# Ranks of two edge sorts: products on TensorE in place of scans on VectorE

## The reference

```python
agg = segment_sum(h_src * attn_weights[:, None], tgt, num_segments=N)      # layer 0, by target
return segment_sum(proj, src, num_segments=n_nodes)                       # layer 1, by source
out = segment_sum(h[src] * alpha[:, :, None], dst, num_segments=N)        # layer 2, by target
mat = mat.at[i].set(c * ri - s * rj); mat = mat.at[j].set(s * ri + c * rj)  # layer 3, edge by edge
return x @ mat.T
```

## Time and profile before

| | |
|---|---|
| median of three runs | 7119.62 us (7114.62 to 7124.22) |
| the profiled execution | 7110.56 us, span 7108.8 us |
| DVE busy, share of the span | 5179.6 us, 73% |
| PE busy | 4283.0 us, 60% |
| POOL busy | 4285.9 us, 60% |
| ACT busy | 1186.0 us, 17% |

### The profile page before, as it was taken

How to read it: one execution, slowest core, us unless ns; L and a number is a source line. 1 busy time by engine, 2 the same in 40 slices (tenths; PEclk the granted TensorE clock), 3 DMA queues, 4 the chain that set the end, 5 groups by cost and what they waited for, 6 DMA issues and landing times. The chain is left out here.

```text
span 7108.8 us, 179388 instructions
## 1 busy us (share of the span) xinstructions
PE 4283.0 (60%) x60437; PEld 3470.5 (49%) x60555; DVE 5179.6 (73%) x12108; ACT 1186.0 (17%) x2828; POOL 4285.9 (60%) x3974
## 2 busy tenths in 40 slices
PE   0000288885425554888887788886888875355541
PEld 0000166663214443677775677764777754233331
DVE  6999877776545556688874688865788855588877
ACT  0000022220011110122220122210222211222210
POOL 5888777776357760477760677741777720677720
PEclk9999999996555556999998999998999987555555
DMA  0000000001044441677722677614777500444420
GB/s 30 1 4 1 1 1 1 1 1 27 11 104 131 131 117 40 196 216 209 211 72 79 194 218 208 193 34 124 208 215 210 149 19 28 96 111 110 111 58 18
DMA packets 708570, 691.60 MB, mean 97 GB/s; under 512 B 234981, under 2 KB 589355, under 8 KB 708165
## 3 DMA queue, kind: packets, MB, share of 16 engines
q0 software_dynamic: 227328, 446.06, 23.1%
q1 hardware_dynamic: 480846, 240.51, 12.2%
HBM read 766.03 MB, written 77.58 MB: 119 GB/s over the span
## 5 line engine op out<-in xcount | busy, mean ns | idle before, releaser
L1671 POOL DMA_INDIRECT kvring<-kvtab,oth x1776 | 1800.4, 1014 | 818.7 <-issue 432.3
L1069 POOL DMA_INDIRECT e_hg<-htab,oth_d x992 | 1012.6, 1021 | 818.7 <-issue 763.6
L1722 PE MATMUL ea_pss<-ea_qb,ea_kT 128*128 128x128 f32 x7104 | 1016.4, 276 | 0.0
L1722 PEld LDWEIGHTS ea_pss<-ea_qb,ea_kT 128*128 128x128 f32 x7104 | 942.4, 193 | 16.0
L1766 ACT ACTIVATE ea_kT<-ea_pst 128x512 f32<-128x512 f32 x888 | 482.0, 595 | 1833.9 <-PE ea_pst L1710 1833.9
L1710 PE MATMUL ea_pst<-ident,kvring 128*128 128x128 f32 x3552 | 484.8, 280 | 306.5 <-DMA kvring<-kvtab,oth 304.6
L241 POOL DMA_INDIRECT steps<-or_rec,or_rplacei x392 | 567.1, 1447 | 135.2 <-issue 121.5
L1806 DVE TENSOR_REDUCE ea_sc<-ea_pss 128x64 f32<-128x1024 f32 x444 | 540.3, 1217 | 47.0 <-PE ea_pss L1722 47.0
L1710 PEld LDWEIGHTS ea_pst<-ident,kvring 128*128 128x128 f32 x3552 | 384.1, 141 | 379.2 <-DMA kvring<-kvtab,oth 213.6
L1834 DVE TENSOR_TENSOR ea_mix<-ea_hot,ea_psg 128x1024 f32<-128x1024 f32 (+1 forms) x444 | 542.2, 1221 | 0.2
L1719 PE MATMUL ea_pss<-mrow,ea_mk 128*128 128x256 bf16 x1776 | 490.2, 276 | 58.0 <-ACT ea_kT L1766 25.7
(11 more groups left out here) (506 smaller groups left out, 8295.2 us busy)
## 6 DMA issues: line engine op xcount, KB each, us to landing
ea_qb<-qtab SPq DMA_DIRECT2D x1776, 64.0 KB
qtab<-at_qst SPq DMA_DIRECT2D x75, 512.0 KB, 3.3
kvring<-kvtab,oth POOLq DMA_INDIRECT x1776
e_stack<-ohtab SPq DMA_DIRECT2D x744, 32.0 KB
kvtab<-at_kvst SPq DMA_DIRECT2D x75, 256.0 KB, 2.7
e_hg<-htab,oth_d POOLq DMA_INDIRECT x992
ea_mk<-mtab SPq DMA_DIRECT2D x444, 3.0 KB
htab<-Hd SPq DMA_DIRECT2D x2, 3200.0 KB, 11.9
```

Of the source, the lines that this page charges most:

```text
L1069: pool.indirect_dma_start(out=hg[:, b % RING, u, :], out_offset=None, in_=htab, in_offset=bass.IndirectOffsetOnAxis(ap=oth[:, b * 4 + u:b ...
L1671: pool.indirect_dma_start(out=kv[:, b % R, u, :], out_offset=None, in_=kvtab, in_offset=bass.IndirectOffsetOnAxis(ap=oth[:, b * QB + u:b * ...
L1722: mm = pe.matmul(ps_s[r % 2][:, u, k * 2 * HN:(k + 1) * 2 * HN], kT[:, r % 2, u, k, :], qb[:, r, u, :], start=False, stop=True, skip_group ...
```

## The change

Both sorts get their ranks from PE.

The first sweep still makes one mask for each block on DVE, now as bf16 (`hot`). For every mask PE forms one product of 392 columns with `colsel`, a matrix whose only column of ones stands so that block u's counts by column land in row u of a PSUM bank; 64 blocks share a bank and are summed there (two banks in turn). After 64 blocks DVE scans the bank once along the columns (`columns`), so 2 scans for the target sort and 4 for the source sort give, for each block, the edges in all earlier columns. The first place of the block is added as a column (`bcol`, turned by a small product), and the sum is split in two bf16 parts (`rows`).

In the second sweep DVE makes the mask, PE forms two products of 392 columns that add up in one PSUM bank, `laterb` by mask (the edges of this block in earlier partitions of the same column) and a selector by `rows` (the block's row, spread over the partitions), and DVE copies the sum, predicated by the mask, from PSUM into the places. Three PSUM banks and three mask buffers are used in turn. Constants for this are set by `sort_constants` on DVE and `sort_selectors` on ACT. `PARTS` becomes (232, 40, 120). The order of the edges within a block is now by columns.

```diff
-PARTS = (272, 32, 88)
+CH = 64
+MIDDLE = 32768.0
+PARTS = (232, 40, 120)
...
+def sort_constants(dve, K, B, s):
+    link = linker(dve, s["sconst"])
+    link(dve.memset(B["colsel"][:, :], 0.0))
+    for at in (CH - 1, 2 * CH - 1):
+        link(dve.memset(B["colsel"][:, at:at + 1], 1.0))
...
+def sort_selectors(act, B, s):
+    act.wait_ge(s["eye2"], 1)
+    act.activation(B["selb"][:, :, :], B["eye2"][:, :].unsqueeze(2).broadcast_to([P, CH, P]), ACT.Copy).then_inc(s["selb"], 1)
...
+    def columns(c):
+        dve.wait_ge(s["cnt"], min(SB, CH * (c + 1)))
+        dve.tensor_tensor_scan(E[:, c, 1:RT], K["ones"][:, 0:1].broadcast_to([P, RT - 1]), ps_c[c % 2][:, 0:RT - 1], 0.0,
+                               ALU.mult, ALU.add).then_inc(s["run"], 1)
...
-        dve.scalar_tensor_tensor(out=run[:, b % 3, :], in0=blk[:, :], scalar=float(b),
+        dve.scalar_tensor_tensor(out=hot[:, b % 3, :], in0=blk[:, :], scalar=float(b),
                                  in1=K["ones"][:, 0:1].broadcast_to(full), op0=ALU.is_equal, op1=ALU.mult,
-                                 accum_out=cnt[:, b:b + 1]).then_inc(s["cnt"], 1)
+                                 accum_out=cnt[:, b:b + 1]).then_inc(s["here"], 1)
+        if b >= CH + 2 and b % CH == 2:
+            columns(b // CH - 1)
...
+    for c in range(NC):
+        link(dve.tensor_scalar(rows[:, c, :], E[:, c, :], bcol[:, c:c + 1], None, ALU.add))
+        dve.scalar_tensor_tensor(out=rows[CH:P, c, :], in0=E[CH:P, c, :], scalar=bcol[CH:P, c:c + 1], in1=rows[CH:P, c, :],
+                                 op0=ALU.add, op1=ALU.subtract).then_inc(s["rows"], 1)
+
     for k in range(SB + 2):
         if k < SB:
             if k >= 3:
                 dve.wait_ge(s["put"], k - 2)
-            dve.tensor_scalar(here[:, k % 3, :], blk[:, :], float(k), None, ALU.is_equal).then_inc(s["here"], 1)
-        if 1 <= k < SB + 1:
-            b = k - 1
-            dve.wait_ge(s["here"], b + 1)
-            dve.tensor_tensor_scan(run[:, b % 3, :], K["ones"][:, 0:1].broadcast_to(full), here[:, b % 3, :],
-                                   til[:, 3, b:b + 1], ALU.mult, ALU.add).then_inc(s["run"], 1)
+            dve.tensor_scalar(hot[:, k % 3, :], blk[:, :], float(k), None, ALU.is_equal).then_inc(s["here"], 1)
         if k >= 2:
             b = k - 2
-            dve.wait_ge(s["run"], b + 1)
+            dve.wait_ge(s["rank"], b + 1)
             if b >= 1:
                 dve.wait_ge(s["put"], b)
-            dve.copy_predicated(place[:, :], here[:, b % 3, :].bitcast(I32), run[:, b % 3, :]).then_inc(s["put"], 1)
+            dve.copy_predicated(place[:, :], hot[:, b % 3, :].bitcast(I16), ps_k[b % 3][:, 0:RT]).then_inc(s["put"], 1)
...
-def sort_offsets(pe, K, B, s):
-    SB, cnt = B["SB"], B["cnt"]
-    pe.wait_ge(s["cnt"], SB)
-    pe.matmul(B["ps_o"][:, 0:SB], K["later"][:, :], cnt[:, :], start=True, stop=True)
+def sort_ranks(pe, K, B, s, selectors):
+    SB, NC, cnt, hot, ps_c, ps_k = (B[n] for n in ("SB", "NC", "cnt", "hot", "ps_c", "ps_k"))
+    for b in range(SB):
+        c, u = b // CH, b % CH
+        pe.wait_ge(s["here"], b + 1)
+        if u == 0 and c >= 2:
+            pe.wait_ge(s["run"], c - 1)
+        pe.matmul(ps_c[c % 2][:, 0:RT], B["colsel"][:, CH - 1 - u:CH - 1 - u + P], hot[:, b % 3, :], start=(u == 0),
+                  stop=(u == CH - 1 or b == SB - 1)).then_inc(s["cnt"], 1)
     pe.matmul(B["ps_n"][:, 0:SB], K["ones"][:, :], cnt[:, :], start=True, stop=True).then_inc(s["offs"], 1)
...
+    for b in range(SB):
+        c, u = b // CH, b % CH
+        if u == 0:
+            pe.wait_ge(s["rows"], c + 1)
+        pe.wait_ge(s["here"], SB + b + 1)
+        if b >= 3:
+            pe.wait_ge(s["put"], b - 2)
+        pe.matmul(ps_k[b % 3][:, 0:RT], B["laterb"][:, :], hot[:, b % 3, :], start=True, stop=False)
+        pe.matmul(ps_k[b % 3][:, 0:RT], B["selb"][:, u, :], B["rows"][:, c, :], start=False, stop=True).then_inc(s["rank"], 1)
```

More of the change, by code:

```diff
@@ L11 @@
 I32 = mybir.dt.int32
+I16 = mybir.dt.int16
 P = 128
@@ L136, in loop_linker @@
     return link
-def sort_prepare(dve, K, B, s):
[L141 to L145, removed]
+def sort_constants(dve, K, B, s):
[3 more added lines that the diff above has]
+        link(dve.memset(B["colsel"][:, at:at + 1], 1.0))
+    link(dve.memset(B["tt"][:, :, :, :].rearrange("p c a b -> p (c a b)"), 0.0))
+    link(dve.memset(B["E"][:, :, 0:1], 0.0))
+    link(dve.tensor_copy(B["laterb"][:, :], K["later"][:, :]))
+    dve.tensor_tensor(B["eye2"][:, :], K["ident"][:, 0:CH], K["ident"][:, CH:P], ALU.add).then_inc(s["eye2"], 1)
+def sort_selectors(act, B, s):
+    act.wait_ge(s["eye2"], 1)
+    act.activation(B["selb"][:, :, :], B["eye2"][:, :].unsqueeze(2).broadcast_to([P, CH, P]), ACT.Copy).then_inc(s["selb"], 1)
+def sort_prepare(dve, K, B, s):
+    W, T, SB, TG, NC, full = B["W"], B["T"], B["SB"], B["TG"], B["NC"], [P, RT]
+    i_t, blk, place, placei, rawrec, padrec, hot = (B[n] for n in ("i_t", "blk", "place", "placei", "rawrec", "padrec", "hot"))
+    E, rows, tt, bcol, ps_c, ps_k, ps_b = (B[n] for n in ("E", "rows", "tt", "bcol", "ps_c", "ps_k", "ps_b"))
+    cnt, til, til_i, tcol, bt, bti, junk, ps_n = (B[n] for n in ("cnt", "til", "til_i", "tcol", "bt", "bti", "junk", "ps_n"))
     link = linker(dve, s["chain"])
+    def columns(c):
+        dve.wait_ge(s["cnt"], min(SB, CH * (c + 1)))
+        dve.tensor_tensor_scan(E[:, c, 1:RT], K["ones"][:, 0:1].broadcast_to([P, RT - 1]), ps_c[c % 2][:, 0:RT - 1], 0.0,
+                               ALU.mult, ALU.add).then_inc(s["run"], 1)
     link(dve.tensor_scalar(i_t[:, :], B["key"][:, :], W.bit_length() - 1, None, ALU.logical_shift_right))
@@ L151, in sort_prepare @@
             dve.wait_ge(s["cnt"], b - 2)
-        dve.scalar_tensor_tensor(out=run[:, b % 3, :], in0=blk[:, :], scalar=float(b),
+        dve.scalar_tensor_tensor(out=hot[:, b % 3, :], in0=blk[:, :], scalar=float(b),
                                  in1=K["ones"][:, 0:1].broadcast_to(full), op0=ALU.is_equal, op1=ALU.mult,
-                                 accum_out=cnt[:, b:b + 1]).then_inc(s["cnt"], 1)
+                                 accum_out=cnt[:, b:b + 1]).then_inc(s["here"], 1)
+        if b >= CH + 2 and b % CH == 2:
+            columns(b // CH - 1)
+    for c in range((SB - 3) // CH, NC):
+        columns(c)
     link(dve.tensor_scalar(i_t[:, :], B["key"][:, :], W - 1, None, ALU.bitwise_and))
@@ L182, in sort_prepare @@
     dve.tensor_scalar(bti[:, :], bt[:, :], float(SB - 1), None, ALU.min).then_inc(s["tiles"], 1)
-    dve.wait_ge(s["cnt"], SB)
+    dve.wait_ge(s["base"], 1)
+    link(dve.tensor_copy(bcol[:, 0:NC], ps_b[:, 0:NC]))
+    dve.wait_ge(s["run"], NC)
+    for c in range(NC):
+        link(dve.tensor_scalar(rows[:, c, :], E[:, c, :], bcol[:, c:c + 1], None, ALU.add))
+        dve.scalar_tensor_tensor(out=rows[CH:P, c, :], in0=E[CH:P, c, :], scalar=bcol[CH:P, c:c + 1], in1=rows[CH:P, c, :],
+                                 op0=ALU.add, op1=ALU.subtract).then_inc(s["rows"], 1)
     for k in range(SB + 2):
@@ L208, in sort_prepare @@
     dve.sem_inc(s["placed"], 1)
-def sort_offsets(pe, K, B, s):
-    SB, cnt = B["SB"], B["cnt"]
-    pe.wait_ge(s["cnt"], SB)
-    pe.matmul(B["ps_o"][:, 0:SB], K["later"][:, :], cnt[:, :], start=True, stop=True)
-    pe.matmul(B["ps_n"][:, 0:SB], K["ones"][:, :], cnt[:, :], start=True, stop=True).then_inc(s["offs"], 1)
+def sort_ranks(pe, K, B, s, selectors):
[7 more added lines that the diff above has]
+                  stop=(u == CH - 1 or b == SB - 1)).then_inc(s["cnt"], 1)
+    pe.matmul(B["ps_n"][:, 0:SB], K["ones"][:, :], cnt[:, :], start=True, stop=True).then_inc(s["offs"], 1)
+    pe.wait_ge(s["tt"], NC)
+    for c in range(NC):
+        mm = pe.matmul(B["ps_b"][:, c:c + 1], B["tt"][:, c].rearrange("p a b -> p (a b)"), K["ident"][:, 0:1],
+                       start=True, stop=True, skip_group_check=True)
+    mm.then_inc(s["base"], 1)
+    pe.wait_ge(selectors, 1)
+    for b in range(SB):
[7 more added lines that the diff above has]
+        pe.matmul(ps_k[b % 3][:, 0:RT], B["selb"][:, u, :], B["rows"][:, c, :], start=False, stop=True).then_inc(s["rank"], 1)
 def sort_store(sp, B, s):
@@ L849, in order_and_rotate @@
             ps_y=pb("psy", [P, D]))
-        temps = dict(i_t=sb("i_t", full, I32), blk=sb("blk", full), place=sb("place", full), here=sb("here", [P, 3, RT]),
-                     run=sb("run", [P, 3, RT]))
+        NC = -(-NP // NBS // CH)
+        bank = lambda v, dims: v.rearrange(f"p {dims} -> p ({dims})")
+        temps = dict(i_t=sb("i_t", full, I32), blk=sb("blk", full), place=sb("place", full), hot=sb("hot", [P, 3, RT], BF16),
+                     E=sb("E", [P, NC, RT]), rows=sb("rows", [P, NC, RT], BF16), tt=sb("tt", [P, NC, 2, CH]), bcol=sb("bcol", [P, NC]),
+                     colsel=sb("colsel", [P, CH - 1 + P], BF16), laterb=sb("laterb", [P, P], BF16), eye2=sb("eye2", [P, CH]),
+                     selb=sb("selb", [P, CH, P], BF16),
```

(11 more changed lines are left out.)

11 lines of the change are left out of this document (7 added, 4 removed).

## The result

The changed kernel takes 6939.14 us (median of four runs, 6927.73 to 6945.87) against 7120.77 us of the kernel before (four runs, 7114.62 to 7124.22): ratio 0.9745, interval 0.9729 to 0.976. The forecast was 6945 us. The profiled execution took 6927.73 us, span 6925.9.

A forecast was written before the change was run, and what follows sets the result against it. DVE's sorts and POOL's list scatters set the rotation's start, with POOL the later after the change. A start 223 us earlier less 48 us handed on gives -175 us: 6936 profiled, 6945 us timed, range 6920 to 7040.

The forecast's parts named there:

- The likeliest case: Whole kernel: 6945 us; with free scatters and the small end of a PE-bound sweep (6925 to 6970), chance 0.66.
- Second sweep on DVE: Sorts: without 300 scans a block takes 0.94 us against 1.894, 286 us off DVE, which is through at 554 us.
- Products on PE: Sorts' second sweep: two products of 392 columns per block at 0.43 us each, 0.86 us, still under DVE's 0.94.
- rival that PE sets the sweep: Second sweep: products take 1.49 us per block, rotation from 723 us, kernel 7064 us; PE-bound further up, chance 0.09.
- serial hand-over: Second sweep: DVE, PE, DVE without overlap, 2.16 us per block, rotation from 924 us, kernel 7265 us; chance 0.04.
- Scatters beside the second sweep: POOL in the sorts: only the compare blocks scatters, 1.33 us each, 212 done there; list ends at 597 us.
- rival with free scatters: Second sweep: the compare costs POOL nothing, 1.27 us per scatter, rotation from 592 us, 6933 us; chance within the forecast's 0.66.
- The hand-over to the rotation: List's end to rotation's start: 2.7 us until the last scatter lands plus 4.15 us of fetch; start at 604 us.
- The rotation: DVE's stage after the sorts: length stays 841 us, ending at 1445 us, with POOL just fitting near 1436 us.
- What POOL hands on: Source scatters moved to later stages: 8 us more in the table stage, 40 in the type counts, together +48 us.
- Sum: Whole kernel: -223 us at the rotation's start plus 48 us handed on gives -175 us; everything behind the type counts unchanged.
- locked-scatters rival: Second sweep: the copy from PSUM still blocks POOL, 1.88 us per scatter, rotation from 683 us, 7024 us; chance 0.17.

## Why the prediction was right

The likeliest case came true, 6 us from its time. By its own steps:

- *Second sweep on DVE: right.* 0.957 us per block against 0.94, DVE through at 556.6 us against 554. The copy from PSUM cost 20 ns more than that from SBUF, and the compare's wait gives 0.24 us in four blocks.
- *Products on PE: right that they hide, mis-sized.* Two products stand 0.30 us apart (421.03 and 421.33), and 0.33 us where the first ones of a sweep stand back to back, not 0.43: the price by columns, taken from products of 192, was too high. They did begin at the low level, as the forecast took it, although the row of that stretch shows 1.00. Only two copies waited for PE (0.9 us in all). The rival that PE sets the sweep did not come, and the four-product run moved it further away than argued. The serial hand-over did not come either: on DVE compare and copy follow each other without idle time.
- *Scatters beside the second sweep: the mis-sized step.* "A scatter meets it about one time in three for half its length" gave 1.33 us; it is 1.28, the size of the rival with free scatters. The step had the compare hold up POOL; in the rows it is the compare that is held up (0.60 us), and the scatters keep 0.97. The list's last scatter ended at 592.4 us instead of 597.
- *The hand-over to the rotation* took 4.5 us (592.4 to 596.9), not the 6.85 us summed up from a landing and a fetch; in the run with the copy from SBUF it was 4.8, with the ones in PSUM 4.6. Both together make the start 7 us earlier than the 604 us foretold.
- *The rotation* took 837.0 us against 841. In the experiments' profiles it took 838.1 to 844.7 us (843.3, from 578.89 to 1422.2 us, with the ones in PSUM), so 4 us are no finding.
- *What POOL hands on: 47.2 us against 48*, with two errors that cancel. The table stage grew from 50.1 to 61.9 us (8 foretold): the scatters took 10.5 us more and began 1.0 us later, and little of the slack was there. The type counts grew from 151.0 to 186.4 us, 35.4 instead of 40: POOL works 41.6 us longer there, but the stage ends 2.3 us after POOL's last scatter where it was 8.8 before. That tail goes with the split, not the sorts: 2.3 us again in the kernel before with the new split, 8.8 again in the changed one with the old split. What ends it was not looked into.
- *Sum:* -230.1 - 4.4 + 47.2 = -187.3 us at the start of the stage behind, as the first view shows. The rest of the program gave 4.5 us back; in the ten profiles it took 5237 to 5259 us, so that is its scatter. That the total comes within 6 us is in part luck: a start 7 us early and a rotation 4 us short stand against these 4.5 us.
- *The locked-scatters rival* fell by the third view. What remained of it in the run with the copy from SBUF was 28 us, not the 79 us between 7024 and 6945.

## What to carry to other kernels

Where GpSimd issues scatters beside VectorE, list the VectorE instructions of that stretch by how many operands they read from SBUF: one with two is paid for on GpSimd's side, and moving a constant operand to PSUM can be the cheapest cure (here some 50 us of 6939 for two such operands). The count of operands is not all: the compare of the second sweep reads one, and still every fourth of them was held up by 0.24 us, here on VectorE's side. Before shortening an engine's block, ask which of the engines ends the stage last after the change; a split of work between stages that costs 46 us beside one bottleneck costs nothing beside another. A price taken from products at the low granted clock was an upper bound here: twice as many products were granted the high level.

## What the runs showed that was not expected

The wait between DVE and POOL can fall on either engine. Before, it fell mostly on POOL: scatters took 1600 ns, and the mask compare 0.45 us (170 of the 175 in the window of the earlier trace rows), against 0.33 to 0.36 us for four others. After, scatters keep 972 ns and every fourth compare takes 0.60 instead of 0.36 us, so that four blocks lock to three scatters (with bf16 input the long compares take 0.42 instead of 0.26 us). The long compares start 0.56 us after a scatter's start (421.51 against 420.95); those that start 0.04 or 0.41 us after one aren't longer. The Trainium skill, page "SBUF — State Buffer", section "Who interferes with whom", has it that of a GpSimd instruction and a VectorE instruction in a two-port mode, whichever issued first has the shared ports for the whole instruction and the other waits. The long compares agree that the later one waits; the compares at 0.04 and 0.41 us, which also run beside a scatter and are not longer, do not agree with the whole instruction. That this compare runs in such a mode is not shown here.

The granted clock rose when PE had more to do: 0.60 and 0.53 in the second sweeps with two products per block, 1.00 and 0.99 with four, in the same two windows of 94 and 189 us. And a shown clock of 1.00 need not tell the products' speed: in the first sweep, with one product every 0.49 us, it is 1.00 from 70 to 120 us and 0.50 from 230 to 331, but all the 192 products into the first bank are recorded with 506 to 511 ns. The four-product run shows it by starts: the first 16 products of the target sort's second sweep (131.32 to 136.18 us) start 0.33 us apart, those of one block from 136.42 us on 0.17 us, and the windows of 131 to 135 and of 140 to 150 us both show 1.00.
